# Attention and gated linear attention over 32 tiles: the input also loaded transposed, the layer norm moved into weights and maxima

## The reference

```python
def _layernorm(x, axis=-1, eps=1e-05):
    m = jnp.mean(x, axis=axis, keepdims=True)
    v = jnp.var(x, axis=axis, keepdims=True)
    return (x - m) / jnp.sqrt(v + eps)
...
        q = (x_q @ W_q.T).reshape(b, nq, H, HD)
...
        scores = jnp.einsum('bqhd,bqkhd->bqkh', q, k) * SCALE
        attn = jax.nn.softmax(scores, axis=2)
...
    x = x + _L0_xattn_ref(_layernorm(x, axis=-1), ctx_1024, itok_BxSx64_0_2047, L0_xattn_W_q, L0_xattn_W_kv_down, L0_xattn_W_kv_up, L0_xattn_W_out)
```

## Time and profile before

| | us |
|---|---|
| median of 3 runs | 1115.98 |
| lowest and highest run | 1109.65 and 1116.11 |
| span of the profiled execution | 1110.1 |
| mean granted TensorE clock, share of full speed | 0.982 |

### The profile page before, as it was taken

How to read it: one execution, slowest core, us unless ns; L and a number is a source line. 1 busy time by engine, 2 the same in 40 slices (tenths; PEclk the granted TensorE clock), 3 DMA queues, 4 the chain that set the end, 5 groups by cost and what they waited for, 6 DMA issues and landing times.

```text
span 1110.1 us, 30832 instructions
## 1 busy us (share of the span) xinstructions
PE 1057.4 (95%) x11840; PEld 879.0 (79%) x11840; DVE 981.3 (88%) x2793; ACT 905.9 (82%) x2259; POOL 683.0 (62%) x707
## 2 busy tenths in 40 slices
PE   3789999999999999999999999999999999999985
PEld 2567888888888888888888888888888888888764
DVE  5779999999999999999999999999999999998643
ACT  3588888888888888888888888888888888888752
POOL 5366665566676556667665576766567676654553
PEclk8789999999999999999999999999999999999989
DMA  5432221223222222223221122222212222211111
GB/s 153 150 127 57 75 78 50 54 57 84 63 69 70 54 56 57 75 60 88 69 59 46 49 74 67 75 72 70 54 53 64 58 69 70 68 37 47 26 32 25
DMA packets 86856, 73.82 MB, mean 67 GB/s; under 512 B 34553, under 2 KB 71743, under 8 KB 86710
## 3 DMA queue, kind: packets, MB, share of 16 engines
q1 hardware_dynamic: 86134, 70.85, 24.2%
q10 hardware_dynamic: 576, 1.02, 0.3%
HBM read 37.43 MB, written 13.94 MB: 46 GB/s over the span
## 4 chain that ended last, share of the span: by engine, by line
PE 83%; DVE 7%; DMA 3%; POOL 3%; ACT 2%; SPq 1%; issue 1%; ACTq 0%; DVEq 0%; POOLq 0%
PE F L403 10%; PE TM L738 6%; PE F L874 6%; PE F L885 5%; PE F L822 5%; PE F L397 5%; PE F L849 5%; PE F L790 4%; PE F L805 3%; PE F L879 3%; PE SA L726 3%; PE F L1113 3%; PE F L763 3%; PE TM L757 3%; PE F L866 3%; PE F L833 3%
## 5 line engine op out<-in xcount | busy, mean ns | idle before, releaser
L733 DVE CUSTOM_DVE_ANT_0 SA<-SA,LNC 128x154 f32<-128x154 f32 x512 | 146.1, 344 | 11.5 <-PE SA L726 9.8
L2168 POOL COPY X1B<-X 128x256 f32<-128x256 f32 x27 | 13.9, 516 | 149.3 <-DVE X L1434 149.3
L738 PEld LDWEIGHTS TM<-CONST,EXPS 128*128 128x128 f32 x512 | 74.5, 208 | 27.3 <-issue 24.8
L719 DVE TENSOR_REDUCE PACKED<-HOT 128x19 int32<-128x1216 bf16 x64 | 92.3, 1443 | 0.0
L738 PE MATMUL TM<-CONST,EXPS 128*128 128x128 f32 x512 | 89.8, 299 | 2.3 <-ACT EXPS L1769 1.3
L733 DVE DVE_READ_ACCUMULATOR2_ANT MAXS<- 128x1 f32 x512 | 70.0, 137 | 0.0
L874 PE MATMUL F<-QM,STATE 128*64 128x128 f32 x1024 | 64.7, 280 | 2.9 <-POOL QM L2229 1.8
L874 PEld LDWEIGHTS F<-QM,STATE 128*64 128x64 f32 x1024 | 56.8, 139 | 13.3 <-POOL QM L2195 8.3
L2163 POOL TENSOR_TENSOR LS<-LS,ZABS 128x1024 f32<-128x1024 f32 x27 | 63.9, 2366 | 4.7 <-ACT ZABS L1914 3.8
L885 PE MATMUL F<-WO,OG 128*128 128x256 f32 x256 | 63.6, 391 | 2.2 <-DVE OG L1524 2.0
L403 PEld LDWEIGHTS F<-XMT,WQ 128*128 128x128 f32 x512 | 63.9, 196 | 1.8
(11 more groups left out here) (536 smaller groups left out, 3840.8 us busy)
## 6 DMA issues: line engine op xcount, KB each, us to landing
QD<-QG SPq DMA_DIRECT2D x128, 128.0 KB, 2.3
QS<-q_dram SPq DMA_DIRECT2D x64, 192.0 KB, 3.1
q_dram<-QPARTS SPq DMA_DIRECT2D x32, 192.0 KB, 2.2
XA<-x_dram SPq DMA_DIRECT2D x32, 128.0 KB, 2.2
QS<-q_dram SPq DMA_DIRECT2D x32, 128.0 KB, 3.1
XB<-x_dram SPq DMA_DIRECT2D x32, 128.0 KB, 3.0
out_dram<-OUT SPq DMA_DIRECT2D x32, 128.0 KB, 1.7
EG<-EGP SPq DMA_DIRECT2D x128, 4.0 KB, 1.8
```

Of the source, the lines that this page charges most:

```text
L719: return dve.tensor_reduce(PACKED[:, r], HOT[:, r, :], AX.X, ALU.add)
L733: last = dve.tensor_tensor_reduce(s, s, LNC[t % 2][:, :], -1.0, LARGE, ALU.add, ALU.min, out[:, h:h + 1])
L738: pe.transpose(TA[:, cols(hh)], exps[:, 0:P, hh], ident)
```

## The change

The host gives the input a second time as xT, each tile transposed. It is loaded to XT and multiplied by the query weights without being normalised. The mean is taken out by centring the weights: at setup TensorE multiplies WQ_A by a matrix of 1/256 and VectorE subtracts the result from WQ_A. The division by the deviation is put off: the raw scores are multiplied by minus the reciprocal deviation in the maxima instruction, which takes it as a per-partition operand where it had the constant -1.0, and since LNC is added before that, the logarithm of the counts is multiplied by the deviation on GpSimd first. XN, its transposes and XNT are gone. Semaphores are renamed and regrouped, and a number of waits that other waits imply are taken out; a few are put in.

```diff
-        RSTD = sb("RSTD", [P, 2])
-        XN = sb("XN", [P, D])
-        XNT = sb("XNT", [P, KD, P])
+        RSTD = [sb(f"RSTDA{i}", [P, 4]) for i in range(3)]
+        XT = sb("XT", [P, KD, P])
...
+            pool.memset(MEANS[:, :], 1.0 / D).then_inc(s_means, 1)
...
+        def pe_centre():
+            pe.wait_ge(s_wq, 16)
+            pe.wait_ge(s_means, 1)
+            for k in range(KD):
+                last = pe.matmul(spare[:, 0:D], MEANS[:, :], WQ_A[:, k, :], start=k == 0, stop=k == KD - 1)
+            last.then_inc(s_wq_means, 1)
+
+        def dve_centre():
+            dve.wait_ge(s_wq_means, 1)
+            dve.tensor_tensor(WQ_A[:, :, :], WQ_A[:, :, :], spare[:, 0:D].unsqueeze(1).to_broadcast([P, KD, D]),
+                              ALU.subtract).then_inc(s_wq_centred, 1)
...
-                    last = pe.matmul(spare[:, cols(m)], WQ_A[:, k, cols(m)], XNT[:, k, :], start=k == 0, stop=k == KD - 1)
+                    last = pe.matmul(spare[:, cols(m)], WQ_A[:, k, cols(m)], XT[:, k, :], start=k == 0, stop=k == KD - 1)
...
-                last = dve.tensor_tensor_reduce(s, s, LNC[t % 2][:, :], -1.0, LARGE, ALU.add, ALU.min, out[:, h:h + 1])
+                last = dve.tensor_tensor_reduce(s, s, LNC[t % 2][:, :], RSTD[t % 3][:, 3:4], LARGE, ALU.add, ALU.min, out[:, h:h + 1])
...
-            if l < TILES:
-                pe.wait_ge(s_a_xn, l + 1)
-                transposes(spare, XN[:, :], KD).then_inc(s_a_xt_ps, 1)
...
-            dve.tensor_scalar(XN[:, :], XA[:, :], MV[:, 0:1], RSTD[:, 1:2], ALU.subtract, ALU.mult).then_inc(s_a_xn, 1)
...
-            act.wait_ge(s_a_xt_ps, a + 1)
-            act.activation(XNT[:, :, :], spares, ACT.Copy).then_inc(s_a_xt, 1)
...
-                act.activation(RSTD[:, 1:2], RSTD[:, 0:1], ACT.Exp, scale=-0.5).then_inc(s_a_rstd, 1)
+                act.activation(RSTD[l % 3][:, 2:3], RSTD[l % 3][:, 0:1], ACT.Exp, scale=-0.5).then_inc(s_a_rstd, 1)
+                act.activation(RSTD[l % 3][:, 1:2], RSTD[l % 3][:, 0:1], ACT.Exp, scale=0.5)
+                act.wait_ge(s_a_rstd, 2 * l + 2)
+                act.activation(RSTD[l % 3][:, 3:4], RSTD[l % 3][:, 2:3], ACT.Copy, scale=-1.0)
...
-            pool.wait_ge(s_a_off, b + 1)
-            pool.tensor_tensor(LNC[b % 2][:, :], LN[:, :], OFF[:, :], ALU.add).then_inc(s_a_counts_pool, 1)
+            pool.tensor_scalar(LNC[b % 2][:, :], LN[:, :], RSTD[b % 3][:, 1:2], None, ALU.mult).then_inc(s_b_lnc_counts_pool, 1)
+            pool.wait_ge(s_b_lnc_counts_pool, 2 * b + 1)
+            pool.tensor_tensor(LNC[b % 2][:, :], LNC[b % 2][:, :], OFF[:, :], ALU.add).then_inc(s_b_lnc_counts_pool, 1)
...
         def sp_first_tiles(l, a, b, c, d, e):
             if l >= 1:
-                sp.wait_ge(s_a_xn, l)
+                sp.wait_ge(s_a_ln, 2 * l - 1)
             sp.dma_start(XA[:, :], x[rows(l), :]).then_inc(s_l_load_xa, 16)
             if l >= 1:
-                sp.wait_ge(s_a_index, 5 * l - 4)
+                sp.wait_ge(s_a_q_ps, l)
+            sp.dma_start(XT[:, :, :], xT[l]).then_inc(s_l_load_xt, 16)
             sp.dma_start(IDX[:, :], idx[rows(l), :]).then_inc(s_l_load_idx, 16)
...
                 sp.dma_start(IDX[:, :], idx[rows(l), :]).then_inc(s_l_load_idx, 16)
-                sp.wait_ge(s_a_xn, l)
                 sp.dma_start(XA[:, :], x[rows(l), :]).then_inc(s_l_load_xa, 16)
+                sp.wait_ge(s_a_q_ps, l)
+                sp.dma_start(XT[:, :, :], xT[l]).then_inc(s_l_load_xt, 16)
             sp.wait_ge(s_d_exp2, 2 * d + 1)
...
         "x": a("x").reshape(B * L, D),
+        "xT": a("x").reshape(TILES, P, KD, P).transpose(0, 3, 2, 1),
```

More of the change, by code:

```diff
@@ L261, in program @@
-        s_a_counts_pool = sem("a_counts_pool")
+        s_b_b = sem("b_b")
+        s_b_b_2 = sem("b_b_2")
+        s_b_b_3 = sem("b_b_3")
+        s_b_exps = sem("b_exps")
+        s_b_exps0_0 = sem("b_exps0_0")
+        s_b_exps0_2 = sem("b_exps0_2")
+        s_b_exps1_0 = sem("b_exps1_0")
+        s_b_exps1_3 = sem("b_exps1_3")
+        s_b_exps2_1 = sem("b_exps2_1")
+        s_b_exps2_3 = sem("b_exps2_3")
+        s_b_exps_2 = sem("b_exps_2")
+        s_b_exps_ps = sem("b_exps_ps")
+        s_b_lnc_counts_pool = sem("b_lnc_counts_pool")
@@ L301, in program @@
         s_c_router_z = sem("c_router_z")
-        s_c_rexp = sem("c_rexp")
+        s_c_rows_ps = sem("c_rows_ps")
+        s_c_rstd = sem("c_rstd")
+        s_c_sg = sem("c_sg")
+        s_c_sigm = sem("c_sigm")
+        s_c_silu = sem("c_silu")
+        s_c_soft = sem("c_soft")
+        s_c_v = sem("c_v")
+        s_c_v_ps = sem("c_v_ps")
+        s_c_xm = sem("c_xm")
+        s_c_xmt = sem("c_xmt")
+        s_c_xmt_ps = sem("c_xmt_ps")
         s_c_z0_ps = sem("c_z0_ps")
-        s_c_zabs = sem("c_zabs")
+        s_c_z1_ps = sem("c_z1_ps")
@@ new lines, in program @@
+        s_c_zslabs = sem("c_zslabs")
+        s_c_zstore = sem("c_zstore")
+        s_d_a1_ps = sem("d_a1_ps")
+        s_d_a2_ps = sem("d_a2_ps")
+        s_d_at = sem("d_at")
+        s_d_at1 = sem("d_at1")
+        s_d_at2 = sem("d_at2")
+        s_d_dec = sem("d_dec")
+        s_d_egd = sem("d_egd")
+        s_d_en2 = sem("d_en2")
+        s_d_exp1 = sem("d_exp1")
+        s_d_exp2 = sem("d_exp2")
+        s_d_g2_ps = sem("d_g2_ps")
+        s_d_k1 = sem("d_k1")
+        s_d_k1t_ps = sem("d_k1t_ps")
@@ L331, in program @@
+        s_d_k2gt_ps = sem("d_k2gt_ps")
+        s_d_k2t_ps = sem("d_k2t_ps")
+        s_d_kg2 = sem("d_kg2")
+        s_d_kvd_ps = sem("d_kvd_ps")
+        s_d_ms_ps = sem("d_ms_ps")
+        s_d_norm = sem("d_norm")
+        s_d_o_ps = sem("d_o_ps")
+        s_d_osg = sem("d_osg")
+        s_d_q1 = sem("d_q1")
+        s_d_q1_ps = sem("d_q1_ps")
+        s_d_q2 = sem("d_q2")
         s_d_q2_ps = sem("d_q2_ps")
-        s_d_k2t_ps = sem("d_k2t_ps")
-        s_d_q2 = sem("d_q2")
         s_d_qd = sem("d_qd")
@@ L931, in pe_first_tiles @@
             if b >= 0:
-                scores(b, 2).then_inc(s_b_scores, 1)
+                scores(b, 2).then_inc(s_b_b_2, 1)
             if d >= 0:
@@ L958, in pe_first_tiles @@
                 pe.wait_ge(s_b_exps0_2, b + 1)
-                scores(b, 3).then_inc(s_b_scores, 1)
+                scores(b, 3).then_inc(s_b_b_3, 1)
             if c >= 0:
```

552 lines of the change are left out of this document (225 added, 327 removed).

## The result

The changed kernel takes 1139.08 us (median of 4 runs, 1136.26 to 1143.17), the kernel before 1115.19 in the runs beside it. The ratio on record is 1.0237, 95% interval 1.0206 to 1.0268; the two medians alone give 1.0214. That is slower by 24 to 26 us, where 1120 was forecast and 1131 was the end of the range. A repetition gave 1.0235 (1.0201 to 1.0269). The median of the kernel before differs by up to 0.4% between the sets of runs, so what follows compares ratios, each taken against runs of before made beside it.

A forecast was written before the change was run, and what follows sets the result against it. TensorE was taken to bound the kernel, with the other engines a little ahead. Against a span of 1110.1 us, 3 + 3.5 + 2 + 1.5 = +10 gave 1120 us; own range 1112 to 1126, wider range 1105 to 1131.

The forecast's parts named there:

- TensorE's gain: Steady turns: TensorE loses the transposes of XN, gaining 0.21 us a turn, bounds 0 and 0.38.
- the reordered waits: Semaphore waits taken out on VectorE, ScalarE and TensorE stood where another engine was awaited anyway: 0.
- SyncE's queue: XT's load waits for the query product, making EG moves 1.1 us late; about +0.05 us a turn by this path.
- What would show it: Signs listed: EG 1.1 us later, GpSimd waiting for EG, TensorE for QM, maxima near 0.40 us, first scores near 27.
- VectorE: Maxima 68 ns dearer each (bounds 0 to 79), XN's 0.32 us returned; biting at the next scores: +0.1 us a turn.
- GpSimd's multiplication: One 128x154 multiplication before LNC, hidden behind 2.9 us; would cost 0.5 if that cover went.
- The fill: Filling turns: first scores +3.5 us from centring and XT's wait, next turn +2, turns 3 to 5 +1.5.
- the turn behind it: Fill's next turn: weight loads and query parts' store behind XT's third load, partly covered: +2 us, between 0 and 5.
- A: Rival: SyncE's wait and the maxima both covered, turns 0.21 us shorter, fill costs 3 to 4: 1108 us; chance 0.25.
- C: Rival: clearly faster, removed waits and the shorter way to the query product close up the filling turns: 1096 us; chance 0.08.
- B: Rival: VectorE becomes the bound through the dearer maxima, each of 27 turns 0.5 us longer: 1130 us; chance 0.22.
- the +3 for the turns: Steady turns: +0.1 us for each of 27, the larger of the VectorE and GpSimd paths, not their sum.

The follow-up runs named there:

- e1_two: The changed kernel with two XT tiles, so XT's load waits for the query product of a turn earlier: ratio 1.0059.
- e5_all: The changed kernel with two XT tiles, no centring, the constant -1.0 in the maxima and log counts unscaled: ratio 0.9950.
- e12_centre: The changed kernel with two XT tiles, the constant -1.0 in the maxima and log counts unscaled, but the centring kept: ratio 0.9966.
- e6_before_xt: The kernel before with one more 128 KB load a turn, into a tile nobody reads, at XT's place and behind the same wait for the query product: 1.0236.
- e3_const: The changed kernel with the constant -1.0 back in the maxima, leaving out the reciprocal deviation there: ratio 1.0215.
- e9_two_act: The changed kernel, computation complete, with two XT tiles and the log counts scaled on ScalarE instead of GpSimd: ratio 1.0054.
- e4_plain: The changed kernel without GpSimd's multiplication of the log counts, which are added as they are: ratio 1.0242.
- e8_xt_later: The changed kernel, one XT tile, with XT's load in the fill moved behind the index and context loads: ratio 1.0243.
- e11_xt_behind: The changed kernel, one XT tile, its load and wait moved behind the EG moves in steady turns, behind the query parts' store in the fill: 1.0081.
- e10_exp_scale: The changed kernel, complete: two XT tiles, log counts scaled on ScalarE, constant in the maxima, deviation in the exponentials, one added VectorE scaling a group: 1.0894.

## Why the prediction was wrong, point by point

**TensorE's gain** was forecast at 0.21 a turn. With the other terms taken away the quiet turn is 32.08 for 32.20: 0.12. The missing 0.09 is as much as the mean squares (L1098) wait longer for VectorE's STATE: 0.15 us in every quiet turn of after, e1_two, e5_all and e12_centre, 0.06 before. The prediction had the reordered waits at nothing; no run undid them by themselves, so they are a candidate for it and no more.

**SyncE's queue.** This step failed, and it holds most of the loss. It was forecast at "about +0.05 a turn by this path"; the 26 turns are on average 0.31 us longer in after than in e1_two (32.88 for 32.57), and 0.64 longer in e6_before_xt than in before (32.87 for 32.24). The lateness was right: 1.1 forecast, 1.03 found. So was that TensorE is barely touched by it in a usual turn, forecast +0.05, found 0 to 0.05 in the quiet turns of e6_before_xt. Wrong were two sentences. "The fourth starts near 571.8 and lands 1.8 later" took one turn's issue and landing for every turn's, although has landings up to 2.1, and the whole trace of before has EG landings up to 3.1 and one EG issue of 1.64 us. In the long turns of after with a late EG the four issues stretch by up to 1.1, or the last landing by up to 1.7, and a slack of 0.7 us does not cover that. And "The QD moves, HIDK and the z stores also go 1.1 us later; their readers come some microseconds after" was not followed to the last link: store, landing, load, landing, and TensorE's z products, which turned out to wait longest of all: 4.0 us in after and 8.5 in e6_before_xt. The "What would show it" named GpSimd's wait for EG and TensorE's for QM, and both came in the long turns only (in a quiet one GpSimd stands 0.1 us for EG).

**VectorE.** The price per maximum was forecast at 68 ns and is 35 (344 to 379), in the lower half of the bounds. The built-in operations of the earlier trace rows did not carry over to this custom one. Yet the maxima cost 0.26 a turn, not 0.1: the bite is not at the scores of the fourth group. The path that ends last goes on to QG at L1423, for which TensorE's L830 waits 0.12 us in quiet turns and not at all before; L813 waits another 0.05 for KG1T, and e3_const has neither wait. Ahead of QG stand two groups, eight maxima of 0.035: 0.28. That this is the place is read from the traces; the 0.26 is measured.

**GpSimd's multiplication** was costed at nothing, "hidden behind 2.9 us". Its own end was hidden, but it moved the addition onto VectorE's scan: 0.17 a turn, which would be 4.4 us in 26 turns (3.9 from e1_two to e9_two_act, in the traces). The Trainium skill (SBUF — State Buffer, Who interferes with whom) states this: a VectorE instruction with two inputs in SBUF and a GpSimd instruction that reads SBUF exclude each other, and the second waits for the first. The scan reads two tiles in SBUF, the maxima one and PSUM. The trace agrees in kind: the scan takes 0.85 us for 0.68 where it meets the addition, though the two overlap by 0.30, and the maxima take 379 ns with the multiplication and 378 without (e4_plain). The prediction did not weigh that rule.

**The fill** was forecast at +7 and is +10.6 at the sixth product (8.4 in the repetition). The first scores came at 30.00, not 27, the next tile's first scores at 53.36 for 43.73. "Three loads and after them the key stores" was too small: the load of the other context was among the three, and TensorE stood 5.5 us for it at the head of its own list. But e1_two, in which that wait is gone, has its first scores at 27.83, so XT's wait is 2.2 us of their lateness, and what else made them late in it is regained by the sixth product (149.68 for 150.37). Timeline of TensorE in after:

```profile
12.69 1.92 PE L717 MATMUL F<-XT,WQ_A 128*128 128x128 f32 x8
20.07 3.45 PE L605 MATMUL F<-CTXT,WDOWN 128*128 128x462 f32 x4 [5.47 <-DMA CTXT<-ctxT_dram]
30.00 0.67 PE L734 MATMUL SA<-KNOW,QS 128*128 128x154 bf16 x4 [4.77 <-DMA QS<-q_dram]
...
53.36 0.69 PE L734 MATMUL SA<-KNOW,QS 128*128 128x154 bf16 x4 [4.04 <-DMA QS<-q_dram]
```

The larger part lies in the turn behind it, forecast at "+2, between 0 and 5" because "the whole row of issues moves 4 to 5 us". The third query product comes at 62.48 in after and at 53.84 in e1_two, 8.6 apart where the second were 2.2 apart; the fourth are 11.4 apart, the sixth 11.3. SyncE in after, then in e1_two:

```profile
37.04 0.35 SPq L2188 DMA_DIRECT2D XT<-xT_dram  x1
...
37.91 0.43 SPq L449 DMA_DIRECT2D WA<-wa_dram  x1
...
44.43 0.51 SPq L2231 DMA_DIRECT2D q_dram<-QPARTS  x1
49.33 1.25 SPq L723 DMA_DIRECT2D QS<-q_dram  x3
```

```profile
24.33 0.43 SPq L449 DMA_DIRECT2D WA<-wa_dram  x1
...
38.91 0.38 SPq L2233 DMA_DIRECT2D q_dram<-QPARTS  x1
41.48 1.25 SPq L723 DMA_DIRECT2D QS<-q_dram  x3
```

XT waits for the product to end, and the nine weight loads, the store of the query parts and the loads of QS stand behind it. The first weight load went out at 26.68 before and the store at 34.60; they go out 11.2 and 9.8 us later, not 4 to 5. e8_xt_later, which frees the context load and leaves this place as it is, and e11_xt_behind, which frees both, show that it is here: their third products come at 60.13 and 54.76, their sixth at 158.6 and 151.0.

Behind that, between 50 and 75 us, the granted clock of TensorE is on average 0.66 in after, 0.84 in before and 1.00 in e1_two. In after it is 0.50, the lower level of 1.2 GHz, from 53 to 70 us; TensorE had just stood idle for 4.04 us for QS. For the same 18.8 us of busy time after gets 102 instructions done and e1_two 172, so the late start seems to be paid at a lower clock as well; no run separates the two.

**The rivals.** A (both covered) and C fell with the result. B named the nearest number, 1130, by a mechanism that isn't the cause: with the maxima back at their old price the ratio is still 1.0215, and without the multiplication it is 1.0242. The 2.4% are 1.8 by the queue (e1_two against after) and 1.1 by maxima, multiplication and centring (e5_all against e1_two), less the 0.5 that the change gains. This split depends on the order in which the terms are taken out: the waiting load alone costs the kernel before 2.4% (e6_before_xt), since turns that wait for the queue hide the other terms. That the direction was right is in part luck: the +3 for the turns was put down to the scores of VectorE's fourth group, which was not the place, and the queue's path in the turns, which holds most of the loss, was given almost nothing.

**What is open.** In e6_before_xt three long turns (32.60 to 33.06) have neither a late EG nor a lengthened issue of EG or QD. That a code load lengthens the issues beside it is read from coincidence in all these traces; no run moved the code loads by themselves. The stretch behind the last query product is 2.8 us shorter in after, and all runs but e10_exp_scale spread over 118.4 to 121.5 there without a pattern.

## What to carry to other kernels

A wait that is added to an in-order DMA queue is paid by everything behind it, through store, landing, reload and reader: follow each of these chains to the engine that ends last, and measure its slack against the worst issue and landing in the trace, not the usual ones. A single-buffered load belongs behind the moves that are in a hurry, in the fill's list as well; that recovered nearly as much as a second buffer (1.0081 for 1.0059). Where several small costs share a turn, read the quiet turns too: the ratios of the single edits e3_const and e4_plain could not be told from after's, while the distance from turn to turn showed 0.26 and 0.17 us.

## What the runs showed of the hardware

- Code loads of up to 16 KB run beside the kernel's own moves on DMA queues of their own (q8: 93 loads, 1.52 MB in an execution). Where one starts among SyncE's issues, an issue of 0.61 us takes up to 1.70 in after and 2.09 in e1_two, and moves of EG land up to 3.5 us after their issue in after, 3.7 in the repetition, instead of 1.8. The loads drift through the turn, and the long turns come in groups where they pass the moves of EG and QD.
- The custom maximum over 154 columns takes 344 to 346 ns with a constant and 379 with a per-partition operand.
- A VectorE tensor_scalar of 4 columns from SBUF to SBUF takes 0.23 us, and up to 1.7 when it starts within a GpSimd instruction: each of the 60 lengthened ones ends 0.02 to 0.03 us after that one's end. By the same section of the Trainium skill a tensor_scalar may take both ports and, where GpSimd came first, is shut out while it runs; the trace agrees, and shows it at 4 columns too.
